# A fused Mamba and feed-forward kernel: z's products around x, softplus without a clamp, u for two tiles at once, and a loop written out

## The chip, the cores and the metric

The kernel runs on one core of one Trainium2 chip. The metric is the device time of one execution in microseconds. The kernel before was timed three times: 2849.44 us at the median, 2845.27 to 2853.36.

## The reference, cut to what matters

The input x has 2 sequences of 2048 rows of 512 numbers. A small recurrence with 64 states gives y0; its layer norm feeds a Mamba block, and a feed-forward block follows (second phase of the kernel, not touched by the change). In the Mamba block, with 1024 inner channels and 16 states each:

```python
xz = xn @ W_in
x_br, z = jnp.split(xz, 2, axis=-1)
xb = jax.nn.silu(conv(x_br) + conv_b)          # causal, 4 taps
Bm = xb @ W_b;  Cm = xb @ W_c
delta = jax.nn.softplus(xb @ W_delta + b_delta)
A_bar = jnp.exp(delta[..., None] * A)
Bx = delta[..., None] * Bm[:, :, None, :] * xb[..., None]
h = A_bar * h + Bx                             # scan over time
y = jnp.sum(h * Cm[:, None, :], axis=-1) + xb * Dp
out = y * jax.nn.silu(z) @ W_out
```

The kernel's u is delta * xb, so that Bx = u * B.

## The kernel before

**Tiling.** Time is cut into NBLK = 16 blocks of T = 256 columns (two sequences in turn), the channels into ND = 8 tiles dt of 128 partitions, the 16 states of a tile into 4 groups g of G = 4. A step k of `scan_phase` works on three blocks at once: it scans block k (`scan`), makes xb, z, B, C and delta of block k + 1 (`front`), and finishes block k - 1 (`back`). Steps run from k = -1 to 16. Each step has NQ = 32 slots q = 4 * dt + g, and each engine has its own written order of jobs by slot: the table `plan` on PE, `next_plan`, `scan_plan`, `turned` and `back_plan` on ACT, `next_plan` and `scan_plan` on DVE.

**A slot.** ACT writes the decay factors exp(delta * A) of group q to PSUM (L659; called exp(q) below; two buffers, so exp(q) waits for scan q - 2). DVE multiplies u by B into a ring of 4 buffers (`bx`, L836, one slot ahead; it waits until PE has turned state q - 4) and scans (`scans`, L844). POOL saves the carry (L445) and multiplies by C in two halves (L452). PE turns the states by transposes that add in PSUM (`turn_states`, L1041). At g = 0 DVE first computes u of the tile in PSUM (L818) and writes column 0 of B (L833, L829). In slots q % 4 = 1 DVE multiplies a finished tile by silu(z) (`gate`, L782), and `turn_gated` (L1051) on PE and `gT` (L592) on ACT turn a pair of such tiles back.

**The next block's work.** PE has two PSUM banks, `work[0]` and `work[1]`, for its products. The order of their users is the order of the table `BANK`; `give(job)` waits until the user before has been copied out. In slots q = 12 to 18 PE makes x (`x(j, m)`, L980, 4 taps each) and z (`z(j)`, L988), ACT copies them out (`xcopy`, L539; `zcopy`, L532) and applies silu to x (L548) before it copies z. `bc` (L996) needs silu of x, then `dl` (L1007) makes delta's argument v in four pairs of tiles.

**Softplus.** It is max(v, ln(1 + min(e^v, CAP))): `dexp` on ACT makes e^v into `lnbuf` (L574) and v into `delta` (L576); `dmin` on DVE clamps `lnbuf` (L765); `dln` on ACT takes Ln(x + 1) (L582); `dmax` on DVE takes the maximum (L772).
**The loop.** `run_steps` runs steps -1, 0, 15 and 16 with constants and steps 1 to 14 as a loop of 7 turns with two steps each, on every engine; SP, which issues the DMAs, loops over steps 1 to 12. In the loop the values waited for are computed in registers from the loop variable.

## Time and profile before

| | |
|---|---|
| median of 3 runs | 2849.44 us |
| profiled execution | 2850.96 us, its span 2848.9 us |
| first scan to last scan | 116 to 2327.6 us of the span |
| second phase | 2327.6 to 2848.9 us |
| busy | PE 2387.0, DVE 2361.8, ACT 1680.4, POOL 1679.7 us |
| granted TensorE clock, mean | 0.915 of 2.4 GHz |

A row of a timeline is: start and duration in us, engine, line, operation, output <- inputs, shape, number of instructions merged into it, and in brackets the idle time of the engine before it with what ended it.
### The profile page before, as it was taken

What the parts mean: (1) busy time and instruction counts of PE and PEld (TensorE: products, weight loads), DVE (VectorE), ACT (ScalarE), POOL (GpSimd) and SP (SyncE); (2) the same over time, 40 slices, a digit from 0 to 9 for tenths busy, and PEclk for the clock granted to TensorE, in tenths of its full rate; (3) what the DMA queues carried; (4) which work ended last, traced back from release to release, by engine and by line L of the source; (5) the groups of instructions that cost most, each with busy time, mean ns of one, the idle gap of its engine ahead of it and who ended that gap; (6) DMA issues with size and microseconds to landing.
All of it is one profiled execution on the core that took longest, in us unless ns stands there. A gap on an engine that the chain in (4) does not pass through costs nothing. (4 is left out here: it accounts for less than half of the span.)

```text
span 2848.9 us, 38192 instructions
## 1 busy us (share of the span) xinstructions
PE 2387.0 (84%) x11520; PEld 1647.4 (58%) x11520; DVE 2361.8 (83%) x2454; ACT 1680.4 (59%) x3282; POOL 1679.7 (59%) x1993
## 2 busy tenths in 40 slices
PE   7878888888878888888888878888888794999997
PEld 5556666565757575757565657565666331444443
DVE  2489898989898989898989899988989664788886
ACT  2566656565756575756575656666666334555554
POOL 0277677767676767676677677676767550223231
PEclk8889999999999898999899999898998896999999
DMA  4101020202020101011010102020102532111110
GB/s 173 67 2 69 7 71 5 72 5 74 2 76 9 68 16 61 19 57 47 30 54 22 62 16 68 8 69 8 60 9 89 216 132 79 49 67 59 62 59 23
DMA packets 47510, 152.50 MB, mean 54 GB/s; under 512 B 7973, under 2 KB 8869, under 8 KB 44206
## 3 DMA queue, kind: packets, MB, share of 16 engines
q1 hardware_dynamic: 47278, 149.76, 14.7%
q8 instruction: 102, 1.67, 0.3%
q14 instruction: 130, 1.06, 0.1%
HBM read 132.37 MB, written 17.37 MB: 53 GB/s over the span
## 5 line engine op out<-in xcount | busy, mean ns | idle before, releaser
L452 POOL TENSOR_TENSOR ring<-ring,Cbc 128x512 f32<-128x512 f32 x1024 | 1290.8, 1282 | 44.2
L844 DVE TENSOR_TENSOR_SCAN ring<-a_ps,ring 128x1024 f32<-128x1024 f32 x512 | 1165.0, 2278 | 25.9 <-ACT a_ps L659 25.9
L659 ACT ACTIVATE a_ps<-delta,nA 128x255 f32<-128x255 f32 x2048 | 854.3, 467 | 506.1 <-DVE ring L844 505.2
L1041 PE MATMUL yT_ps<-ident,ring 128*128 128x128 f32 x4096 | 613.4, 295 | 215.4 <-POOL ring L452 188.6
L1041 PEld LDWEIGHTS yT_ps<-ident,ring 128*128 128x128 f32 x4096 | 501.3, 151 | 320.0 <-POOL ring L452 257.4
L836 DVE TENSOR_TENSOR ring<-u_ps,Bbc 128x1024 f32<-128x1024 f32 x512 | 621.0, 1213 | 76.7 <-PE yT_ps L1041 69.6
L445 POOL TENSOR_TENSOR carry<-ring,half 128x4 f32<-128x4 f32 x512 | 145.2, 284 | 599.0 <-DVE ring L844 595.1
L1007 PE MATMUL work<-xb,big 128*128 128x256 f32 x2048 | 482.2, 389 | 0.0
L1007 PEld LDWEIGHTS work<-xb,big 128*128 128x128 f32 x2048 | 392.6, 197 | 51.3 <-issue 0.4
L980 PE MATMUL work<-y0s,big 128*128 128x256 f32 x1024 | 240.6, 392 | 1.2 <-ACT y0s L512 1.2
L1023 PE MATMUL work<-Wout,xb 128*128 128x512 f32 x512 | 241.3, 607 | 0.0
L1381 POOL TENSOR_TENSOR m<-m,pows 128x1 f32<-128x1 f32 x64 | 34.2, 549 | 310.9 <-DVE m L1513 310.9
L980 PEld LDWEIGHTS work<-y0s,big 128*128 128x128 f32 x1024 | 199.0, 198 | 29.9 <-ACT y0s L512 1.5
L1023 PEld LDWEIGHTS work<-Wout,xb 128*128 128x128 f32 x512 | 98.4, 199 | 112.2 <-issue 112.2
L988 PE MATMUL work<-big,y0s 128*128 128x512 f32 x128 | 85.8, 781 | 67.8 <-ACT zs L532 67.8
L539 ACT ACTIVATE xb<-work,V 128x256 f32<-128x256 f32 x128 | 53.7, 471 | 133.8 <-PE work L980 133.8
L1448 PE MATMUL o_ps<-q,qhT 128*128 128x512 bf16 x512 | 119.3, 387 | 11.8 <-DVE qhT L1546 11.8
L1412 PE MATMUL x_ps<-lay,x2T 128*128 128x512 f32 x256 | 122.0, 621 | 0.7 <-ACT x2T L1473 0.7
L1427 PE MATMUL h_ps<-q,qaT 128*128 128x512 bf16 x512 | 115.7, 379 | 0.0
L574 ACT ACTIVATE lnbuf<-work,V 128x256 f32<-128x256 f32 x128 | 60.4, 472 | 87.2 <-PE work L1007 87.2
L1479 ACT ACTIVATE hb<-hb 128x2048 f32<-128x2048 f32 x32 | 61.2, 1912 | 65.5 <-DVE hb L1532 65.5
L1532 DVE SCALAR_TENSOR_TENSOR hb<-h_ps,m,b1r 128x2048 f32<-128x2048 f32 x32 | 75.2, 2350 | 27.6 <-PE h_ps L1427 27.6
(194 smaller groups left out, 2581.7 us busy)
## 6 DMA issues: line engine op xcount, KB each, us to landing
Bbc<-bc_rows SPq DMA_DIRECT2D x64, 512.0 KB, 4.7
Cbc<-bc_rows SPq DMA_DIRECT2D x64, 512.0 KB, 3.8
xT<-in_xT SPq DMA_DIRECT2D x16, 514.0 KB, 3.2
x_rows<-x2row SPq DMA_DIRECT2D x32, 256.0 KB, 2.0
xp<-x_rows SPq DMA_DIRECT2D x32, 256.0 KB, 2.7
xx<-in_x SPq DMA_DIRECT2D x32, 256.0 KB, 2.9
out_rows<-orow SPq DMA_DIRECT2D x32, 256.0 KB, 2.0
delta<-in_c_w SPq DMA_DIRECT2D x6, 1024.0 KB, 5.1
```

Of the source, the lines that this page charges most:

```text
L445: nc.gpsimd.tensor_tensor(carry[:, par, dt, G * g:G * g + G].rearrange("p (g o) -> p g o", o=1), h[:, :, T - 1:T], ident1, ALU.mult).then_ ...
L452: nc.gpsimd.tensor_tensor(hp, hp, Cbc[:, G * g + GP * c:G * g + GP * c + GP, :], ALU.mult)\
L659: r = nc.scalar.activation(a_ps[q % 2][:, i, 1:T], delta[:, par, dt, 1:T], ACT.Exp, scale=nA[:, dt, s:s + 1])
L836: dve.tensor_tensor(ring[:, q % RING, :, :], u_ps.rearrange("p (a t) -> p a t", a=1).to_broadcast([P, G, T]), Bbc[:, G * g:G * g + G, :], ...
L844: dve.tensor_tensor_scan(ring[:, q % RING, :, :].rearrange("p g t -> p (g t)"), a_ps[q % 2][:, :, :].rearrange("p g t -> p (g t)"), ring[: ...
L980: r = pe.matmul(ps[:, T * m:T * m + T], Mx[:, tap, c:c + P], y0s[:, fp, tap:tap + T], start=(tap == 0), stop=(tap == 3))
L1007: r = pe.matmul(ps[:, T * m:T * m + T], Wd[:, d, c:c + P], xb[:, fp, d, :], start=(d == 0), stop=(d == ND - 1))
L1023: r = pe.matmul(ps[:, :], xb[:, fp, d, P * tt:P * tt + P], Wout[:, d, :], start=False, stop=(d == ND - 1))
L1041: r = pe.matmul(yT_ps[:, tt, :], ring[:, q % RING, i, P * tt:P * tt + P], ident[:, :], is_transpose=True, start=False, stop=(g == NG - 1 a ...
L1412: r = pe.matmul(x3_ps[:, :], x2T[:, d, :], lay[:, batch, d, :], start=(d == 0), stop=(d == KD - 1))
L1427: r = pe.matmul(h_ps[:, 512 * c:512 * c + 512], qaT[:, d, :], q1[:, d, 512 * c:512 * c + 512], start=(d == 0), stop=(d == KD - 1))
L1448: r = pe.matmul(o_ps[:, :], qhT[:, d, :], q2[:, d, :], start=(d == 0), stop=(d == KF - 1))
```

## The change

z(0) and z(1) are made before x, right behind `turn_gated(0)`; z(2) and z(3) stay in slots 17 and 18; the parts of x move back by up to one slot and a half; ACT copies z(0) and z(1) in slot 14 and z(2), z(3) behind silu. `prj` is spread over three slots. Softplus becomes relu(v) + ln(1 + exp(-|v|)): `dexp` makes |v| and relu(v), a new ACT function `dtail` applies exp(-x) to the whole of `lnbuf`, `dmin` is gone, and the maximum becomes an addition. u is made for two tiles in one instruction at the even tiles. The steps of the loop are written out on all engines.

```diff
-        "XB0": 0, "XB1": 1, "XB2": 0, "XB3": 1, "Z0": 0, "Z1": 1, "Z2": 0, "Z3": 1, "GT1": 1, "BC": 1, "DL0": 0,
+        "Z0": 0, "Z1": 1, "XB0": 0, "XB1": 1, "XB2": 0, "XB3": 1, "Z2": 0, "Z3": 1, "GT1": 1, "BC": 1, "DL0": 0,
...
-        u_ps = u_full[:, 0:T]
+        u_ps = u_full[:, :].rearrange("p (m t) -> p m t", m=2)
...
-            with eng.Fori(0, (NBLK - 2) // 2) as i:
-                step(2 * i + 1, 1, True, True, True)
-                step(2 * i + 2, 0, True, True, True)
+            for k in range(1, NBLK - 1):
+                step(k, k % 2, True, True, True)
...
-            with sp.Fori(0, (NBLK - 4) // 2) as i:
-                step(2 * i + 1, 1, True, True, True)
-                step(2 * i + 2, 0, True, True, True)
+            for k in range(1, NBLK - 3):
+                step(k, k % 2, True, True, True)
...
-                        nc.scalar.activation(lnbuf[:, j % 2, T * m:T * m + T], ps[:, T * m:T * m + T], ACT.Exp,
+                        nc.scalar.activation(lnbuf[:, j % 2, T * m:T * m + T], ps[:, T * m:T * m + T], ACT.Abs,
                                              bias=bias).then_inc(s_dexp, 1)
                         r = nc.scalar.activation(delta[:, par if late else fp, mt, :], ps[:, T * m:T * m + T],
-                                                 ACT.Identity, bias=bias)
+                                                 ACT.Relu, bias=bias)
                     r.then_inc(free[BANK[f"DL{j}"]], 1)
+
+                def dtail(pair, late):
+                    b = k if late else n
+                    act.wait_ge(s_dexp, 8 * b + 4 * pair + 4)
+                    nc.scalar.activation(ln_full[:, :], ln_full[:, :], ACT.Exp, scale=-1.0).then_inc(s_dmin, 1)
...
-                next_plan = {5: [prj], 6: [prj_ln], 12: [y0scale], 13: [y0back], 15: [lambda: xcopy(0)],
-                             16: [lambda: xcopy(1)], 17: [lambda: xcopy(2)], 18: [lambda: xcopy(3), silu],
-                             19: [lambda: zcopy(0)], 20: [lambda: zcopy(1), lambda: zcopy(2)], 21: [lambda: zcopy(3)],
-                             22: [bc], 23: [zsilu], 24: [lambda: dexp(0, False)], 26: [lambda: dexp(1, False)],
+                next_plan = {5: [prj], 6: [prj_ln], 12: [y0scale], 13: [y0back], 14: [lambda: zcopy(0), lambda: zcopy(1)], 16: [lambda: xcopy(0)],
+                             17: [lambda: xcopy(1), lambda: xcopy(2)], 18: [lambda: xcopy(3), silu],
+                             19: [lambda: zcopy(2)], 20: [lambda: zcopy(3)],
+                             22: [bc], 23: [zsilu], 24: [lambda: dexp(0, False)], 26: [lambda: dexp(1, False), lambda: dtail(0, False)],
...
-                scan_plan = {1: [lambda: dexp(3, True)], 6: [lambda: dln(1, True)]}
-                turned = {14: 0, 21: 1, 28: 2}
+                scan_plan = {1: [lambda: dexp(3, True), lambda: dtail(1, True)], 6: [lambda: dln(1, True)]}
+                turned = {13: 0, 21: 1, 28: 2}
...
-                def dmin(pair, late):
-                    dve.wait_ge(s_dexp, 8 * (k if late else n) + 4 * pair + 4)
-                    dve.tensor_scalar(ln_full[:, :], ln_full[:, :], CAP, None, ALU.min).then_inc(s_dmin, 1)
...
-                    dve.tensor_tensor(d, d, ln_full[:, :], ALU.max).then_inc(s_delta, 1)
+                    dve.tensor_tensor(d, d, ln_full[:, :], ALU.add).then_inc(s_delta, 1)
...
-                    if g == 0:
+                    if g == 0 and dt % 2 == 0:
...
-                        dve.tensor_tensor(u_ps[:, 1:T], delta[:, par, dt, 1:T], xb[:, par, dt, 1:T], ALU.mult).then_inc(s_u, 1)
+                        dve.tensor_tensor(u_ps[:, :, 1:T], delta[:, par, dt:dt + 2, 1:T], xb[:, par, dt:dt + 2, 1:T],
+                                          ALU.mult).then_inc(s_u, 1)
...
-                        dve.wait_ge(s_u, ND * k + dt + 1)
+                        dve.wait_ge(s_u, ND // 2 * k + dt // 2 + 1)
...
+                        if dt % 2:
+                            dve.wait_ge(s_bx, NQ * k + q)
...
-                                      u_ps.rearrange("p (a t) -> p a t", a=1).to_broadcast([P, G, T]),
+                                      u_ps[:, dt % 2:dt % 2 + 1, :].to_broadcast([P, G, T]),
...
-                             13: [keep_y0], 25: [lambda: dmin(0, False)], 27: [lambda: dmax(0, False)]}
-                scan_plan = {3: [lambda: dmin(1, True)], 7: [lambda: dmax(1, True)]}
+                             13: [keep_y0], 27: [lambda: dmax(0, False)]}
+                scan_plan = {7: [lambda: dmax(1, True)]}
...
-                plan = {0: [("n", prj, 0), ("n", prj, 1)], 1: [("n", prj, 2)],
+                plan = {0: [("n", prj, 0)], 1: [("n", prj, 1)], 2: [("n", prj, 2)],
...
-                        11: [("s", turn_gated, 0, k)], 12: [("n", x, 0, 0), ("n", x, 0, 1)],
-                        13: [("n", x, 1, 0), ("n", x, 1, 1)], 14: [("n", x, 2, 0), ("n", x, 2, 1)],
-                        15: [("n", x, 3, 0), ("n", x, 3, 1)], 16: [("n", z, 0), ("n", z, 1)], 17: [("n", z, 2)],
+                        11: [("s", turn_gated, 0, k)], 12: [("n", z, 0), ("n", z, 1), ("n", x, 0, 0)],
+                        13: [("n", x, 0, 1), ("n", x, 1, 0)], 14: [("n", x, 1, 1), ("n", x, 2, 0)],
+                        15: [("n", x, 2, 1), ("n", x, 3, 0)], 16: [("n", x, 3, 1)], 17: [("n", z, 2)],
```

The wait for the bank of YB, which stood before x, now stands before z(0).

## Rows read from the trace of the kernel before

**Rows 1.** The page, part 1: busy time, share of the span, instructions.

```profile
PE 2387.0 (84%) x11520; PEld 1647.4 (58%) x11520; DVE 2361.8 (83%) x2454; ACT 1680.4 (59%) x3282; POOL 1679.7 (59%) x1993
```

**Rows 2.** Windows, one stretch for a step: steps 3, 8, 9 and 11.

```profile
521.70:661.50 139.80, 117.55 (x574) 88.10 (x573) 124.56 (x110) 86.73 (x186) 97.62 (x116) 0.91 0.11 36
...
1214.50:1351.00 136.50, 115.26 (x574) 86.50 (x573) 124.18 (x109) 86.64 (x186) 97.49 (x116) 0.92 0.12 39
1351.00:1490.90 139.90, 118.58 (x573) 89.62 (x572) 123.59 (x111) 86.64 (x186) 97.65 (x116) 0.90 0.11 38
...
1627.60:1764.40 136.80, 113.26 (x575) 86.23 (x574) 123.54 (x111) 86.52 (x186) 97.59 (x116) 0.95 0.12 41
```

**Rows 3.** Timeline of DVE: end of step 0, of step 8, start of step 9.

```profile
197.47 0.18 DVE L833 TENSOR_REDUCE Bbc<-big 128x16 f32<-128x16 f32 x1 [2.27 <-PE yT_ps L1041]
...
244.39 4.46 DVE L844 TENSOR_TENSOR_SCAN ring<-a_ps,ring 128x1024 f32<-128x1024 f32 x2
...
1346.57 4.46 DVE L844 TENSOR_TENSOR_SCAN ring<-a_ps,ring 128x1024 f32<-128x1024 f32 x2
1352.00 0.43 DVE L818 TENSOR_TENSOR u_ps<-delta,xb 128x255 f32<-128x255 f32 x1 [0.96 <-issue]
```

**Rows 4.** Timeline of PE at the start of step 9.

```profile
1357.19 1.09 PE L1041 MATMUL yT_ps<-ident,ring 128*128 128x128 f32 x8 [3.66 <-issue]
```

**Rows 5.** Groups by line and shape: B's product, Ln, a table load.

```profile
L836 DVE TENSOR_TENSOR ring<-u_ps,Bbc 128x1024 f32<-128x1024 f32 x512 | 621.0, 1213 | 76.7 <-PE yT_ps L1041 69.6
...
L659 ACT ACT_TABLE_LOAD x62 | 79.5, 1283 | 1.1
...
L582 ACT ACTIVATE lnbuf<-lnbuf 128x1024 f32<-128x1024 f32 x32 | 33.7, 1052 | 0.2
```

**Rows 6.** Timeline of DVE in slot q = 3 of step 8.

```profile
1228.06 0.67 DVE L765 TENSOR_SCALAR lnbuf<-lnbuf 128x1024 f32<-128x1024 f32 x1
1228.65 0.43 DVE L818 TENSOR_TENSOR u_ps<-delta,xb 128x255 f32<-128x255 f32 x1
1229.11 0.18 DVE L833 TENSOR_REDUCE Bbc<-big 128x16 f32<-128x16 f32 x1
```

**Rows 7.** Timeline of DVE in step 8, slots 18, 20 and 25.

```profile
1294.56 2.29 DVE L844 TENSOR_TENSOR_SCAN ring<-a_ps,ring 128x1024 f32<-128x1024 f32 x1 [1.48 <-ACT a_ps L659]
...
1299.41 0.18 DVE L833 TENSOR_REDUCE Bbc<-big 128x16 f32<-128x16 f32 x1 [2.24 <-PE yT_ps L1041]
...
1325.56 0.92 DVE L765 TENSOR_SCALAR lnbuf<-lnbuf 128x1024 f32<-128x1024 f32 x1 [1.27 <-ACT lnbuf L574]
...
1326.40 1.21 DVE L836 TENSOR_TENSOR ring<-u_ps,Bbc 128x1024 f32<-128x1024 f32 x1
```

**Rows 8.** Timeline of PE in step 8, slots 12 to 24, and one window.

```profile
1271.34 7.08 PE L980 MATMUL work<-y0s,big 128*128 128x256 f32 x32
...
1288.88 1.88 PE L988 MATMUL work<-big,y0s 128*128 128x512 f32 x4
...
1295.10 2.08 PE L988 MATMUL work<-big,y0s 128*128 128x512 f32 x2 [4.33 <-ACT zs L532]
...
1302.96 3.21 PE L996 MATMUL work<-xb,Wbc 128*32 128x256 f32 x14
...
1324.12 1.91 PE L1041 MATMUL yT_ps<-ident,ring 128*128 128x128 f32 x16
...
1295.10:1301.50 6.40, 5.71 (x14) 3.20 (x15) 4.13 (x5) 4.77 (x11) 2.79 (x3) 0.58 0.00 0
```

**Rows 9.** Timeline of ACT in step 8, slots 18 to 21.

```profile
1287.34 0.84 ACT L539 ACTIVATE xb<-work,V 128x256 f32<-128x256 f32 x2 [1.94 <-PE work L980]
...
1289.55 2.00 ACT L548 ACTIVATE xb<-xb 128x1024 f32<-128x1024 f32 x2
...
1292.86 1.67 ACT L659 ACTIVATE a_ps<-delta,nA 128x255 f32<-128x255 f32 x4
...
1300.85 0.60 ACT L532 ACTIVATE zs<-work 128x512 f32<-128x512 f32 x1 [1.49 <-PE work L988]
```

More of the change, by code:

```diff
@@ L854, in step @@
                         mx_scale()
-                        dve.memset(u_ps[:, 0:1], 1.0).then_inc(s_aclr, 1)
+                        dve.memset(u_ps[:, :, 0:1], 1.0).then_inc(s_aclr, 1)
                         dve.wait_ge(s_mxc, ND)
@@ L972, in x @@
                 def x(j, m):
-                    if j == 0 and m == 0:
-                        pe.wait_ge(free[BANK["YB"]], jobs_before("YB", k) + 1)
-                        if isinstance(k, int) and k == -1:
-                            pe.wait_ge(s_mxc, ND)
                     ps = work[BANK[f"XB{j}"]] if m else give(f"XB{j}")
@@ L985, in z @@
                 def z(j):
+                    if j == 0:
+                        pe.wait_ge(free[BANK["YB"]], jobs_before("YB", k) + 1)
+                        if isinstance(k, int) and k == -1:
+                            pe.wait_ge(s_mxc, ND)
                     ps = give(f"Z{j}")
```

## The prediction

> **What bounds the kernel now.** I read the busy shares first: PE 84%, DVE 83%, the others near 59% [rows 1]. Two engines at about the same share say little, so I cut the span at the ends of the 16 scan steps, which are the ends of the last pair of scans of a step [rows 3], and read each stretch with its granted clock [rows 2]. A step in the middle takes 136.5 us with DVE busy 124.2 and PE 115.3. DVE is therefore the main line, with some 12 us of waits per step. The second phase, behind the scan steps, is not changed.
>
> Then I read DVE's rows with their idle time. In slots q = 0 to 14 it hardly waits. From q = 15 to 25 it waits for PE's turned states, for ACT's exponentials and for the two exponentials that `dmin` clamps [rows 7]. There PE is full: its products run without a pause from 1271.34 to 1290.76 [rows 8], then it idles 4.33 us until ACT has copied z's first product, and ACT copies only behind silu and two table loads [rows 9]. So a step has two parts: DVE sets q = 26 to 31 and 0 to 11, and the chain PE, ACT, PE sets q = 12 to 25.
>
> Last, the step lengths. Step 8 takes 136.5 us, step 9, the first of a turn of the loop, 139.9 [rows 2]. Steps 3, 5, 7 and 13 are like step 9 (139.7 to 139.8), all other looped steps are 136.3 to 136.8, and step 11, also behind a jump, is 136.8 at a clock of 0.95 [rows 2].
>
> **The loop written out.** Six jumps back (before steps 3, 5, 7, 9, 11, 13) go. At a jump DVE stands 0.96 us for "issue" [rows 3] and PE 3.66 us, after which PE starts at half clock [rows 4]. I price the jump by the lengths: 5 steps x (139.8 - 136.55) = 16.3 us, and 0.2 for step 11, 16.5 in all. The low bound is what DVE itself loses at the jump, 6 x 0.96 = 5.8 us, in case the rest is half-clock time that turns up elsewhere; I take 16.5, because the even steps have no jump and are all short. The wait values become constants. Step 0 already has constants: from q = 20's column to its end it takes 248.85 - 197.47 = 51.4 us [rows 3], step 8 takes 1351.03 - 1299.41 = 51.6 [rows 3, 7]. So constants give 0 to 0.2 us per step, and I take 0; the register arithmetic is hidden by the busy engine.
> The Trainium skill ("Runtime: NRT & Kernel Launch", Instruction fetch mechanics) says that fetch runs ahead in sequence and a taken branch away from it stalls. The two stalls agree; by that rule straight code costs nothing extra, and the sum stays.
>
> **DVE: softplus without the clamp.** Two `dmin` go per step. The one in q = 3 costs 1228.65 - 1228.06 = 0.59 us of DVE [rows 6]. The one in q = 25 costs 0.84 and the wait of 1.27 before it, 2.1 us [rows 7]; what is late next is PE's turn of state 22, so this part is worked out below. `max` becomes `add` of the same operands: no row shows an add, the product of 1024 elements takes 1.21 us [rows 5], and I take the add to cost what the maximum did: 0 (-0.1 to 0.1).
>
> **DVE: u for two tiles.** A u costs 1229.11 - 1228.65 = 0.46 us [rows 6], busy 0.43 for 255 elements; the product of 1024 takes 1.21 [rows 5], so an element costs (1.21 - 0.43) / 769 = 1.0 ns and 255 more cost 0.26: 0.72 for a double one. Bounds are one u (0.46) and two (0.92). In q = 0 to 11: +0.27 -0.46 +0.27 -0.46 = -0.4 us. With `dmin` -0.6, so DVE reaches q = 12 1.0 us sooner (0.6 to 1.4). The doubles in q = 15 and 23 lie in waits for PE; the one missing in q = 27 gives 0.46. The new wait of an odd tile is for a product two scans old and holds nothing.
>
> **ACT.** `Exp` becomes `Abs` and `Identity` becomes `Relu`, same sizes: 0. No row shows either; Identity and Copy run between exponentials without a table load, and a load would be 1.28 us [rows 5] (rival 3). Added is `dtail`, an Exp of 128x1024, priced by the Ln of that size, 1.05 us [rows 5]; 0.70 to 1.1. In q = 1 exp(1) is behind it, which scan(1) wants only after scan(0) and a product: hidden. In q = 26 behind it stand exp(26), which DVE's scan(26) needs, and Ln, which DVE's add needs in q = 27. `dmin` began when the last Exp of `dexp` ended, at 1325.56 [rows 7]; Relu 0.35, `dtail` 1.05, exp(26) 1.67, load 1.28 and Ln 1.05 end at 1331.0. DVE, with bx(26) at 1325.2 (below), has gate 0.4, two scans of 2.2 and a product of 1.2 to do and reaches the add at 1332.4. Hidden by 1.4 us; a shift of PE's product shifts both. If the cover is gone, `dtail` costs its 1.05 us.
>
> **PE and ACT: z around x.** All times here are of step 8, with the 1.0 us gained earlier set aside. z(0), z(1) (1.9 us) move in front of x; x(3,1) then ends where z(1) ended, at 1290.76 [rows 8], instead of 1287.3. zcopy(0), zcopy(1) now stand before exp(14) and end about 1273.8, so exp(14) ends 1275.5, before scan(14) starts: hidden by 0.7 us. The cost is silu. xcopy(3) 0.84, load 1.28, silu 2.00, load 1.28, exp(18) 1.67 [rows 5, 9] (7.07 together, and gaps of 0.1) put scan(18) at 1297.9 instead of 1294.56 [rows 7]. Then zcopy(2) 0.58, exp(19) 1.66, zcopy(3) 0.60: 1300.8. z(2) and z(3) no longer wait and are done by 1294.1, but turn_gated(1) is behind z(3) on PE and its bank is free only at 1300.8, formerly 1301.45 [rows 9]. exp(20) and the copy gT(1) then let bc start at 1303.1, formerly 1302.96 [rows 8]. So the 4.33 us wait is replaced by one of 6.7 us at the next product, and bc starts 0.15 us later.
> Clock: behind the 4.33 us idle the stretch 1295.1 to 1301.5 has 0.58 [rows 8], so z(2), turn 16 and z(3) ran mostly at 1.2 GHz. In the new order they run at 2.4 GHz and the slow time falls on turn 17 and on bc (3.64 us at full clock), which nothing hides. At 0.58, some 5.4 of the 6.4 us were slow. As much from 1300.8 on reaches 1306.2, 3.1 us into bc, a loss of 1.5. Bounds: 0, if the clock does not fall, to 3.4, if it stays low for some 9 us. x may also meet slow time sooner: 0.3 (0 to 1).
> The Trainium skill ("TensorE: Matmul & The Clock Gate", Part 1) says that idleness gates the clock and activity releases it. The row agrees, and by it the longer idle speaks against this edit.
> From bc on PE has no pause to q = 25. Turns 22 and 23 ran from 1324.12 on for 1.91 us [rows 8], so turn 22 ended at about 1325.2, and bx(26) started behind `dmin` at 1326.40 [rows 7]. Now bx(26) starts when turn 22 ends, 1.2 sooner but for what PE loses. A step gains 1.0 (before q = 12) + 1.2 + 0.46 (u of q = 27) - 0.15 (bc) = 2.5 us, less the slow time of 1.5 + 0.3: 0.7 us. Bounds: 2.5, and -1.9 with 3.4 + 1 us of slow time.
>
> **prj and the rest.** `prj`'s parts go to q = 0, 1, 2. The load of the next xT on SP starts a slot later, a step before its use; ACT takes prj in q = 5: 0. gT(0) in q = 13 waits for PE until about 1267.3 while scan(11) still runs: 0. Step -1: bc about 2 us sooner, but the table load for Exp now comes after Abs, 1.28 + 0.35 later: 0 (-2 to 2). Step 15 (no z, x): -0.8.
>
> **Sum.** 16.5 + 15 x 0.7 + 0.8 = 27.8 us. Span 2848.9 becomes 2821.1; the profiled run took 2850.96 (2.1 around the span), so 2823.2. That run is 1.5 over the median 2849.44, so 2821.7, rounded 2822.
>
> **Rivals.** (1) The clock doesn't fall behind the longer idle, or falls where work is hidden: 2.5 us per step, 2849.4 - 16.5 - 37.5 - 0.8 = 2795. For: steps with other slow places differ by 3 us (step 11 at 0.95). Against: PE's 4.33 us idle has slow work behind it in step 8, and the new one is longer. (2) Slower: silu is late, in q = 18. PE idles 6.7 us or more before turn_gated(1) and stays slow through bc into `dl`, which DVE waits for. At 3.4 + 1 us of slow time and 1 us by which exp(17), behind xcopy(2), holds back scan(17), a step loses 2.9: 2849.4 - 17.3 + 43.5 = 2876. From a loss of 1.15 us per step on it outweighs the jumps. For: the row of 0.58 [rows 8]. Against: exp(17) has some 1.2 us to spare. (3) The change doesn't do what it says: Abs or Relu cost table loads, two of 1.28 around each `dexp`. In q = 26 the add waits 1.2 us and exp(27) another 0.8: 15 x 2 = 30 us, and we are at 2852. The Trainium skill ("ScalarE: Activation LUTs", Table sets) lists both beside exp, which speaks against this rival. (4) The step's gain is given back in full and only the jumps count: 2832. (5) Straight code stalls on fetch, or the jumps' half-clock time comes back: 5.8 + 11.3 = 17 us, 2832 to 2843.
>
> **Chances.** Forecast 0.42 (2806 to 2832), rival 1 0.18, rival 2 0.08, rival 3 0.06, rival 4 0.14, rival 5 0.12. A measurement tells about 0.3% (8.5 us), so faster means under 2840.9. Faster: 0.42 + 0.18 + 0.14 + 0.07 = 0.81; same: 0.05 of rival 5, 0.04 of rival 3, 0.02 of rival 2 = 0.11; slower 0.08. The range leaves out rivals 2 and 3 and the far end of 1: 2789 to 2845.
>
> **What would show it.** No "issue" wait at a step's start, and all of steps 1 to 14 alike, at 135.8 us. No DVE row for the clamp, four u of about 0.7 us per step. PE without a wait at z, but 6 to 7 us idle before turn_gated(1), and a clock near 0.6 in the stretch behind it. DVE's wait before scan(18) near 5 us. Wrong would be: table loads at the Abs line, steps shorter than 134.5, or bc running at full clock.

## The result and the profile of the changed kernel

| | before | changed |
|---|---|---|
| device time, median (lowest to highest) | 2851.4 us (2845.27 to 2853.76) | 2809.86 us (2808.35 to 2811.09) |
| ratio, 95% interval | | 0.9857 [0.9839, 0.9875] |
| profiled execution | 2850.96 us | 2811.04 us |
| its span, mean granted clock | 2848.9 us, 0.915 | 2808.1 us, 0.922 |

The change makes the kernel 41 us faster. The windows of the changed kernel answer to those of [rows 2]: step 0, step 8, step 9, all of steps 1 to 14, step 15 and the second phase. The columns are the stretch, its length, the busy time (and instructions) of PE, PEld, DVE, ACT and POOL, the granted clock, the share of DMA and GB/s.

```profile
109.00:246.50 137.50, 110.42 (x540) 87.20 (x539) 120.60 (x103) 90.92 (x195) 95.15 (x117) 0.83 0.07 23
1189.60:1325.00 135.40, 114.99 (x577) 86.33 (x577) 122.03 (x105) 88.34 (x188) 97.60 (x116) 0.92 0.13 42
1325.00:1459.30 134.30, 112.69 (x571) 85.27 (x570) 122.06 (x105) 88.23 (x188) 97.69 (x116) 0.94 0.11 41
246.50:2134.80 1888.30, 1593.09 (x8015) 1200.96 (x8014) 1708.49 (x1443) 1236.04 (x2632) 1366.33 (x1611) 0.93 0.12 40
2134.80:2287.10 152.30, 117.37 (x483) 56.96 (x482) 119.48 (x98) 71.28 (x159) 95.38 (x113) 0.87 0.50 184
2287.10:2808.10 521.00, 436.98 (x2113) 214.54 (x2143) 364.27 (x646) 276.29 (x275) 118.73 (x138) 0.94 0.16 55
```

The same windows of the kernel before that were not shown yet: step 0, steps 1 to 14, step 15.

```profile
109.00:248.80 139.80, 111.43 (x551) 88.09 (x550) 123.30 (x110) 89.63 (x193) 95.41 (x117) 0.84 0.07 23
...
248.80:2177.20 1928.40, 1626.14 (x8010) 1225.17 (x8009) 1735.63 (x1528) 1212.64 (x2604) 1366.11 (x1611) 0.92 0.11 39
...
2177.20:2327.60 150.40, 117.24 (x490) 57.08 (x489) 121.18 (x102) 70.44 (x158) 95.43 (x113) 0.88 0.49 187
```

Of the 40.8 us of span, steps 1 to 14 give 1928.4 - 1888.3 = 40.1 and the stretch of step 0 gives 139.8 - 137.5 = 2.3; step 15 takes 152.3 - 150.4 = 1.9 back. The long steps of 139.8 us are gone: steps 1 to 13 now take 134.2 or 134.3 and 135.4 in turn, step 14 takes 136.2.

What took the place of the old waits in slots 17 to 22 stands in three timelines of step 8: DVE, PE and ACT. Square brackets hold the idle time ahead of an instruction and what ended it. PE's last two lines and DVE's last one are of step 9.

```profile
1263.64 2.28 DVE L846 TENSOR_TENSOR_SCAN ring<-a_ps,ring 128x1024 f32<-128x1024 f32 x1
...
1271.99 2.29 DVE L846 TENSOR_TENSOR_SCAN ring<-a_ps,ring 128x1024 f32<-128x1024 f32 x1 [4.96 <-ACT a_ps L662]
...
1283.30 1.22 DVE L838 TENSOR_TENSOR ring<-u_ps,Bbc 128x1024 f32<-128x1024 f32 x1 [2.18 <-PE yT_ps L1043]
...
1417.57 1.23 DVE L838 TENSOR_TENSOR ring<-u_ps,Bbc 128x1024 f32<-128x1024 f32 x1 [1.05 <-PE yT_ps L1043]
```

```profile
1266.52 1.02 PE L990 MATMUL work<-big,y0s 128*128 128x512 f32 x2
...
1274.60 1.12 PE L1053 MATMUL work<-ident,gbuf 128*128 128x128 f32 x4 [7.06 <-ACT zs L530]
...
1277.35 4.88 PE L998 MATMUL work<-xb,Wbc 128*32 128x256 f32 x16
...
1410.00 1.11 PE L1053 MATMUL work<-ident,gbuf 128*128 128x128 f32 x4 [7.06 <-ACT zs L530]
...
1412.75 3.54 PE L998 MATMUL work<-xb,Wbc 128*32 128x256 f32 x15
```

```profile
1264.77 0.84 ACT L537 ACTIVATE xb<-work,V 128x256 f32<-128x256 f32 x2 [2.81 <-PE work L978]
...
1266.98 2.00 ACT L546 ACTIVATE xb<-xb 128x1024 f32<-128x1024 f32 x2
...
1270.30 1.67 ACT L662 ACTIVATE a_ps<-delta,nA 128x255 f32<-128x255 f32 x4
...
1273.97 0.58 ACT L530 ACTIVATE zs<-work 128x512 f32<-128x512 f32 x1
```

ACT does xcopy(3), silu and exp(18) in a row, so DVE stands 4.96 us before scan(18), where it stood 1.48 [rows 7]. z(2) runs without a wait, in 1.02 us where it took 2.08 behind one [rows 8], but PE then stands 7.06 us before turn_gated(1), where it stood 4.33 before z(2) [rows 8]. Behind that idle time bc's sixteen products take 4.88 us in step 8 and 3.76 in step 9 (3.54 for the fifteen shown), and DVE's wait before bx(22) is 2.18 us in the one and 1.05 in the other. That is the whole difference between the two step lengths.

The waits of the whole kernel say the same: total us, times, longest.

```profile
PE work L1053 <- ACT zs L530: 105.9, 15, 7.1
...
DVE ring L846 <- ACT a_ps L662: 77.9, 17, 5.0
```

The groups of the softplus and of u (busy us, mean ns, idle time before):

```profile
L817 DVE TENSOR_TENSOR u_ps<-delta,xb 128x510 f32<-128x510 f32 x64 | 54.7, 855 | 0.0
L662 ACT ACT_TABLE_LOAD x62 | 79.5, 1283 | 1.1
L581 ACT ACTIVATE lnbuf<-lnbuf 128x1024 f32<-128x1024 f32 x32 | 34.3, 1072 | 0.0
```

The table loads are 62 as before [rows 5], so Abs and Relu load nothing. A double u takes 0.855 us in the mean; the first of a step is the slow one (1.43 us in step 8, median of all 0.68).

### The profile page after: what moved, and what is told of

The parts are those of the page before. It is cut to its first block and busy times, and to the rows that moved or that the text cites. A ratio compares the mean times of both kernels' runs of the same rounds, so it can differ in the third digit from the quotient of the medians.

```text
span 2808.1 us, 34215 instructions
## 1 busy us (share of the span) xinstructions
PE 2345.5 (84%) x11488; PEld 1623.8 (58%) x11520; DVE 2330.2 (83%) x2358; ACT 1707.3 (61%) x3314; POOL 1679.8 (60%) x1993
## 5 line engine op out<-in xcount | busy, mean ns | idle before, releaser
L1043 PEld LDWEIGHTS yT_ps<-ident,ring 128*128 128x128 f32 x4096 | 495.4, 149 | 289.1 <-POOL ring L450 253.3
L978 PE MATMUL work<-y0s,big 128*128 128x256 f32 x1024 | 233.1, 380 | 0.0
L978 PEld LDWEIGHTS work<-y0s,big 128*128 128x128 f32 x1024 | 189.4, 190 | 35.3 <-ACT zs L530 10.4
L1053 PE MATMUL work<-ident,gbuf 128*128 128x128 f32 x256 | 51.1, 334 | 123.8 <-ACT zs L530 105.9
L1450 PE MATMUL o_ps<-q,qhT 128*128 128x512 bf16 x481 | 112.0, 386 | 18.9 <-DVE qhT L1548 18.7
L1053 PEld LDWEIGHTS work<-ident,gbuf 128*128 128x128 f32 x256 | 35.6, 169 | 140.8 <-ACT zs L530 118.3
```

What stands on the lines that cost most here:

```text
L978: r = pe.matmul(ps[:, T * m:T * m + T], Mx[:, tap, c:c + P], y0s[:, fp, tap:tap + T], start=(tap == 0), stop=(tap == 3))
L1043: r = pe.matmul(yT_ps[:, tt, :], ring[:, q % RING, i, P * tt:P * tt + P], ident[:, :], is_transpose=True, start=False, stop=(g == NG - 1 a ...
L1450: r = pe.matmul(o_ps[:, :], qhT[:, d, :], q2[:, d, :], start=(d == 0), stop=(d == KF - 1))
```

## The experiments

All kernels but the ones compared by name are timed against the kernel before. Runs 1 to 4 share a chip (before: 2845.1 us), so do 5 to 8 (2843.8) and 9 to 12 (2851.8). For all of them the last columns are of steps 1 to 14 in the profiled execution, divided by 14: the length of a step, DVE's busy time, the rest of the step, in which DVE is idle, and the time at half clock, which is the length times twice what the mean granted clock lacks to 1.

| kernel | median us | ratio, 95% interval | step | DVE busy | DVE idle | half clock |
|---|---|---|---|---|---|---|
| before | 2851.4 | | 137.7 | 124.0 | 13.8 | 21.7 |
| changed | 2809.9 | 0.9857 [0.9839, 0.9875] | 134.9 | 122.0 | 12.8 | 18.5 |
| e1 loop written out alone | 2833.4 | 0.9954 [0.9932, 0.9977] | 136.5 | 124.2 | 12.3 | 20.5 |
| e2 changed, with the loop | 2826.6 | 0.9931 [0.9905, 0.9957] | 136.5 | 122.2 | 14.3 | 20.5 |
| e3 changed, z in its old place | 2780.3 | 0.9768 [0.9734, 0.9801] | 133.1 | 122.1 | 11.0 | 12.7 |
| e4 e1 and z moved | 2883.3 | 1.0128 [1.0094, 1.0161] | 139.9 | 124.2 | 15.8 | 27.3 |
| e5 e1 and softplus | 2832.7 | 0.9958 [0.9936, 0.998] | 136.3 | 122.8 | 13.5 | 19.5 |
| e6 e1 and u | 2828.4 | 0.9958 [0.9943, 0.9973] | 136.3 | 123.6 | 12.7 | 20.2 |
| e7 changed, silu a slot later | 2782.3 | 0.9797 [0.9777, 0.9816] | 133.1 | 122.1 | 11.0 | 13.4 |
| e8 e7 and turn_gated(1) later | 2789.1 | 0.982 [0.9799, 0.9841] | 133.4 | 122.1 | 11.3 | 17.8 |
| e9 changed, idle products | 2798.7 | 0.982 [0.9801, 0.984] | 134.5 | 122.1 | 12.4 | 11.9 |
| e10 e1, idle products | 2828.5 | 0.9924 [0.9905, 0.9942] | 135.8 | 124.2 | 11.6 | 17.3 |
| e11 e5, idle products | 2811.3 | 0.9865 [0.9846, 0.9884] | 135.0 | 122.7 | 12.3 | 15.6 |
| e12 e3, idle products | 2774.5 | 0.9731 [0.9715, 0.9748] | 132.5 | 122.2 | 10.3 | 11.0 |

Where DVE is idle, from the same traces: the mean per step of steps 1 to 14, in us, by the scan that comes next. The last column is the sum of all other places.

| kernel | scans 14, 15 | scan 18 | scan 19 | scans 20, 21 | elsewhere |
|---|---|---|---|---|---|
| before | 1.8 | 1.5 | 2.0 | 1.2 | 7.3 |
| changed | 0.8 | 5.0 | 0.0 | 1.5 | 5.6 |
| e1 | 1.9 | 1.5 | 1.5 | 1.2 | 6.3 |
| e3 | 0.8 | 1.5 | 2.1 | 1.1 | 5.6 |
| e4 | 2.4 | 5.0 | 0.1 | 2.1 | 6.3 |
| e5 | 2.6 | 1.5 | 2.3 | 1.2 | 5.9 |
| e6 | 1.6 | 1.5 | 2.5 | 1.2 | 5.9 |
| e7 | 0.7 | 0.0 | 1.5 | 3.2 | 5.6 |
| e9 | 1.6 | 5.0 | 0.0 | 0.3 | 5.6 |
| e10 | 2.2 | 1.5 | 0.3 | 1.4 | 6.3 |
| e12 | 1.3 | 1.5 | 0.5 | 1.5 | 5.6 |

Ahead of scans 14 and 15 stand PE's first products of x, ahead of scan 18 ACT's exponential behind silu, ahead of scan 19 z's products, ahead of scans 20 and 21 turn_gated(1) and bc. DVE makes the column and the product of a slot one slot ahead, so its wait before bx(22) is in the column of scans 20, 21.

Medians of different chips are not compared without their ratios: from the changed kernel to e7, for one, the medians say 27.6 us and the ratios 0.0060 x 2850 = 17; the profiled spans say 2808.1 - 2779.1 = 29.0.

### The loop, alone and taken back

**e1**, the kernel before with the loop written out:

```
-            with eng.Fori(0, (NBLK - 2) // 2) as i:
-                step(2 * i + 1, 1, True, True, True)
-                step(2 * i + 2, 0, True, True, True)
+            for k in range(1, NBLK - 1):
+                step(k, k % 2, True, True, True)
...
```

> The kernel before with the loop written out and nothing else. Theory of the forecast: six jumps of 3.2 us each (less for one) go and constants give nothing, so 2851.4 - 16.5 = 2835, every step 1 to 14 at 136.5 us, no wait for issue at a step's start. Rival: only DVE's 0.96 us per jump is a true cost and the rest is half-clock time that falls elsewhere: 2851.4 - 5.8 = 2845.6, some steps still near 139.8. Second rival: constants speed every step too: below 2828.

The span goes from 2848.9 to 2832.5 us, by 16.4, and the median from 2845.1 to 2833.4, by 11.7 on this chip, where the kernel before ran between 2829 and 2855 (0.0046 x 2850 = 13 by the ratio). The looped steps are alike within 0.6 us (136.2 to 136.8), as expected; one window, step 8:

```profile
1203.90:1340.40 136.50, 115.81 (x574) 87.32 (x573) 124.14 (x111) 86.41 (x186) 97.40 (x116) 0.92 0.12 41
```

**e2**, the changed kernel with the loop put back (the same lines, the other way round):

> The changed kernel with the loop put back and nothing else. Forecast's theory: the parts add up, the jump costs what it cost before, 2809.9 + 16.5 = 2826, with steps in two lengths 3.2 us apart. Rival: the new order has slack or sets its lengths by half-clock time in another way, so that a jump costs only the 0.96 us of DVE: 2816 or less.

It is 16.8 us slower than the changed kernel by the medians (2826.6 against 2809.9; 0.0074 x 2850 = 21 by the ratios; 2827.2 - 2808.1 = 19.1 by the spans). The jumps thus cost 12 to 16 us in the kernel before and 17 to 21 in the changed one: of one size, and not told apart more finely than that. Two lengths of steps 3.2 us apart were expected and don't show: steps take 135.7 to 137.7 us.

Where the price sits can be read from the kernel before. In its steps 3, 5, 7, 9 and 13 DVE is idle 3.7 us more than in the same steps of e1: 1.2 at the jump itself, 0.7 in slot 3, and 0.9 and 0.7 ahead of scans 15 and 19, which wait for PE. In step 11, behind a jump as well, the last two waits are 0.8 and 1.6 us in all (in e1 1.8 and 1.5), and the step takes only 136.8 us. So most of what a jump costs is lost behind it, in waits for PE.

### z in its old place, and z moved alone

**e3**, the changed kernel with z, x, their copies, gT(0) and prj where they were:

```
-                        11: [("s", turn_gated, 0, k)], 12: [("n", z, 0), ("n", z, 1), ("n", x, 0, 0)],
-                        13: [("n", x, 0, 1), ("n", x, 1, 0)], 14: [("n", x, 1, 1), ("n", x, 2, 0)],
-                        15: [("n", x, 2, 1), ("n", x, 3, 0)], 16: [("n", x, 3, 1)], 17: [("n", z, 2)],
+                        11: [("s", turn_gated, 0, k)], 12: [("n", x, 0, 0), ("n", x, 0, 1)],
+                        13: [("n", x, 1, 0), ("n", x, 1, 1)], 14: [("n", x, 2, 0), ("n", x, 2, 1)],
+                        15: [("n", x, 3, 0), ("n", x, 3, 1)], 16: [("n", z, 0), ("n", z, 1)], 17: [("n", z, 2)],
...
```

> The changed kernel with x, z, their copies, gT(0) and prj in their old places; softplus, u and the written-out loop stay. Theory A (forecast): the move of z trades a PE wait of 4.3 us for one of 7 us, bc starts at the same time, so the move gives nothing or costs its half-clock time; this kernel comes out between 2797 and 2812, with PE waiting 4.3 us before z(2) and DVE 1.5 us before scan(18). Rival B: the move is where the step's gain comes from; this kernel is at 2820 or above.

The kernel is 30 us faster than with z moved (2780.3 against 2809.9; 25 by the ratios), where theory A had 2797 to 2812 and rival B 2820 or more: both missed. The move of z is the part of the change that costs, and more than either allowed. A step of e3, DVE's wait before scan(18), and PE's before z(2):

```profile
1175.90:1309.50 133.60, 113.50 (x575) 85.82 (x573) 122.13 (x105) 88.20 (x189) 97.50 (x116) 0.95 0.12 44
```

```profile
1255.61 2.29 DVE L846 TENSOR_TENSOR_SCAN ring<-a_ps,ring 128x1024 f32<-128x1024 f32 x1 [1.48 <-ACT a_ps L662]
```

```profile
1256.15 1.46 PE L990 MATMUL work<-big,y0s 128*128 128x512 f32 x2 [4.33 <-ACT zs L530]
```

DVE does the same work as in the changed kernel (122.1 us a step) and is idle 1.9 us less. PE's idle time before z(2) is the old 4.33 us, yet z(2) takes 1.46 us behind it and not 2.08 [rows 8], and a step has 12.7 us at half clock, where the changed kernel has 18.5.

**e4**, e1 with the same lines moved the other way:

> The kernel before with the loop written out and x, z, their copies, gT(0) and prj in their new places; softplus and u as before. Theory A: 2835 to 2850, no faster than the written-out loop alone. Rival B: at least 10 us below the written-out loop alone, 2825 or less.

It is 50 us slower than e1 on the same chip, and the only kernel slower than before; 2835 to 2850 was expected, a miss on the same side as e3's. A step, and PE behind its longer wait:

```profile
1228.20:1368.10 139.90, 116.84 (x574) 87.16 (x572) 124.14 (x110) 86.47 (x186) 97.35 (x116) 0.90 0.12 42
```

```profile
1315.67 1.12 PE L1049 MATMUL work<-ident,gbuf 128*128 128x128 f32 x4 [7.06 <-ACT zs L530]
...
1318.42 5.26 PE L994 MATMUL work<-xb,Wbc 128*32 128x256 f32 x16
```

bc takes 5.26 us, 1.6 more than at full clock, and half-clock time rises from 20.5 to 27.3 us a step. DVE's idle time rises by 3.4 us a step, 14 x 3.4 = 48 us: 2.0 of it ahead of scans 18 and 19 together (silu's place), 0.9 ahead of scans 20 and 21 (bc) and 0.5 ahead of scans 14 and 15.

### The two edits of DVE, each alone

**e5**, e1 with Abs, Relu, `dtail` and `add` in the place of Exp, Identity, `dmin` and `max`:

```
-                             13: [keep_y0], 25: [lambda: dmin(0, False)], 27: [lambda: dmax(0, False)]}
-                scan_plan = {3: [lambda: dmin(1, True)], 7: [lambda: dmax(1, True)]}
+                             13: [keep_y0], 27: [lambda: dmax(0, False)]}
+                scan_plan = {7: [lambda: dmax(1, True)]}
...
```

> The kernel before with the loop written out and softplus without a clamp (dexp, dtail, add; no dmin); x, z and u as before. Forecast: 0.6 us from q = 3 and up to 1.2 us from q = 25 per step, 15 steps: 9 to 27 us below the written-out loop alone. Rival (half-clock time takes it back): less than 5 us below it. Second rival: Abs and Relu cost table loads, which the groups would show with more than 62 loads at the exponentials' line.

Its ratio is that of e1, so the forecast of 9 to 27 us missed and the rival of less than 5 holds. DVE works 1.4 us less per step and is idle 1.2 us more: 0.7 more ahead of scan 15, 0.8 more ahead of scan 19 (z's products) and 0.4 less at the place of `dmin`. In slot 15 of the longer steps DVE stands 3.00 us ahead of its column, in e1 2.03 (the rows say issue; on PE the turn that it needs stands behind x's first products). The stretch before it, in which these run, has a clock of 0.69. A step and that stretch of e5, its slot 15, and the slot 15 of e1:

```profile
1205.70:1342.40 136.70, 115.87 (x575) 87.20 (x574) 122.79 (x109) 88.32 (x188) 96.86 (x116) 0.93 0.12 43
...
1255.50:1272.00 16.50, 14.71 (x63) 12.50 (x64) 13.69 (x11) 8.29 (x22) 13.85 (x17) 0.69 0.00 1
```

```profile
1272.19 0.18 DVE L832 TENSOR_REDUCE Bbc<-big 128x16 f32<-128x16 f32 x1 [3.00 <-issue]
```

```profile
1269.98 0.18 DVE L831 TENSOR_REDUCE Bbc<-big 128x16 f32<-128x16 f32 x1 [2.03 <-issue]
```

**e6**, e1 with u for two tiles at once:

```
-                    if g == 0:
+                    if g == 0 and dt % 2 == 0:
...
-                        dve.tensor_tensor(u_ps[:, 1:T], delta[:, par, dt, 1:T], xb[:, par, dt, 1:T], ALU.mult).then_inc(s_u, 1)
+                        dve.tensor_tensor(u_ps[:, :, 1:T], delta[:, par, dt:dt + 2, 1:T], xb[:, par, dt:dt + 2, 1:T],
+                                          ALU.mult).then_inc(s_u, 1)
...
```

> The kernel before with the loop written out and u for two tiles; the rest as before. Forecast: 0.4 us before q = 12 and 0.46 in q = 27, 15 steps: 13 us below the written-out loop alone, and about 1 us more of DVE freed in step 15. Rival: the double u is slower than 0.72 us (its mean in the changed kernel is 0.855) and the rest lies in waits: 0 to 6 us below it.

Again the ratio of e1, so the forecast of 13 us missed and the rival of 0 to 6 holds: DVE works 0.6 us less per step and is idle 0.4 more, of which 1.0 more ahead of scan 19. The two edits alone are worth 0.7 and 5 us by the medians (chips differ; by the ratios nothing either time), together, as e3 has them over e1 on one chip, 53. They don't add up. The half-clock time differs: 19.5 and 20.2 us a step apart, 12.7 together. So does DVE's idle time ahead of scans 14 and 15, where x's products run: 2.6 and 1.6 us apart, 0.8 together.

### silu behind exp(18)

**e7** leaves PE's order as the change has it and moves ACT's xcopy(3) and silu behind exp(18):

```
-                             17: [lambda: xcopy(1), lambda: xcopy(2)], 18: [lambda: xcopy(3), silu],
-                             19: [lambda: zcopy(2)], 20: [lambda: zcopy(3)],
+                             17: [lambda: xcopy(1), lambda: xcopy(2)], 19: [lambda: xcopy(3), silu],
+                             20: [lambda: zcopy(2), lambda: zcopy(3)],
```

> The changed kernel with xcopy(3) and silu behind exp(18) instead of before it, and zcopy(2), zcopy(3) together in slot 20. Theory (what sets slots 18 to 21 is ACT's silu before exp(18)): DVE's wait of 4.96 us before scan(18) goes, one of about 1.1 us comes before scan(19), PE's wait of 7.06 us before turn_gated(1) becomes 5.5, bc starts 1.5 to 2 us sooner: 1 to 2 us per step, 2780 to 2796. Rival (PE's products and their half-clock time set these slots): PE starts bc no sooner and the time stays at 2805 to 2812.

It takes 2782.3 us, within the theory's 2780 to 2796. A step, DVE before scan(19), its wait for an exponential now, and PE before turn_gated(1):

```profile
1173.80:1306.90 133.10, 111.14 (x575) 83.87 (x574) 122.13 (x105) 88.09 (x188) 97.62 (x116) 0.96 0.12 43
```

```profile
1256.18 2.29 DVE L846 TENSOR_TENSOR_SCAN ring<-a_ps,ring 128x1024 f32<-128x1024 f32 x1 [1.43 <-ACT a_ps L662]
```

```profile
1257.20 1.11 PE L1053 MATMUL work<-ident,gbuf 128*128 128x128 f32 x4 [5.47 <-ACT zs L530]
```

So one change in ACT's plan gives back what z's move cost: DVE's 4.96 us before scan(18) is gone and 1.43 before scan(19) and 1.6 before bx(21) come in, PE's 7.06 becomes 5.47, and a step is as short as with z in its old place, no shorter. z's move costs with silu ahead of exp(18) and gains nothing without it. Half-clock time falls too, from 18.5 to 13.4 us a step, so this run changes the order and the clock at once; e9 below changes the clock alone. Whether silu behind exp(18) would also help with z in its old place was not run.

**e8** moves, on top of e7, turn_gated(1) and its copy from slot 18 to the next:

```
-                turned = {13: 0, 21: 1, 28: 2}
+                turned = {13: 0, 20: 1, 28: 2}
...
-                        18: [("n", z, 3), ("s", turn_gated, 1, k)], 19: [("n", bc)],
+                        18: [("n", z, 3)], 19: [("s", turn_gated, 1, k), ("n", bc)],
```

> As the one before, and turn_gated(1) on PE goes behind turn 17 into slot 19, its copy gT(1) on ACT into slot 20. Theory: turn 17 no longer stands behind the wait for zcopy(3), and PE's idle time is cut in two parts, which also leaves less half-clock time in bc: another 0.5 to 1.5 us per step, 2765 to 2790. Rival: turn 17 was never late for DVE and bc waits for the same copy: equal to the one before within 3 us.

PE's idle time before turn_gated(1) shrinks to 3.50 us, and nothing is gained: 2789.1 against 2782.3 on the same chip, inside the stated range but slower where 0.5 to 1.5 us a step were to be gained, so the theory missed, half-clock time 17.8 instead of 13.4 us a step, bc 5.16 us. A shorter wait of PE is not by itself less time at half clock. Why bc is slower behind a wait of 3.50 us than behind 7.06 in the changed kernel's step 9 was not found out.

### Keeping PE at work in its wait

These four kernels compute all that the reference wants and add products of 256 columns into a half of yT's bank that nothing reads. They test whether the clock, and not the order, costs the time: they give PE more to do and take no wait away.

```
-        yT_ps = pb("yT_ps", [P, NT, P])
+        yT_full = pb("yT_ps", [P, 512])
+        yT_ps = yT_full[:, 0:T].rearrange("p (t c) -> p t c", t=NT)
...
+                def warm(n, dt):
+                    wait(pe, s_gate, ND * k + dt)
+                    for _ in range(n):
+                        pe.matmul(yT_full[:, T:2 * T], ident[:, :], Mx[:, 0, 0:T], start=False, stop=False,
+                                  skip_group_check=True)
...
-                        18: [("n", z, 3), ("s", turn_gated, 1, k)], 19: [("n", bc)],
+                        18: [("n", z, 3), ("w", warm, 13, 4), ("s", turn_gated, 1, k)], 19: [("n", bc)],
```

**e9**, the changed kernel with thirteen of them before turn_gated(1), as above:

> The changed kernel with 13 products of 256 columns (5.8 us, into the unused half of yT's PSUM bank, read by nobody) put on PE behind z(3), in the 7.06 us in which it waits for zcopy(3). Theory (half-clock time behind this idle stretch is what the move of z costs): bc runs at full clock and each step is 0.5 to 1.5 us shorter, 2786 to 2804, though PE has 78 us more work. Rival (the order of the waits costs it): work added to PE gives nothing or delays, 2808 or more.

It takes 2798.7 us, 11 less than the changed kernel by the medians and by the ratios. The stretch of bc, PE, and DVE at bx(22):

```profile
1270.00:1276.00 6.00, 5.36 (x30) 3.24 (x31) 6.00 (x4) 3.94 (x11) 5.10 (x6) 1.00 0.00 0
```

```profile
1262.87 5.78 PE L1052 MATMUL yT_ps<-big,ident 128*128 128x256 f32 x26
...
1270.09 0.66 PE L1060 MATMUL work<-ident,gbuf 128*128 128x128 f32 x4 [1.45 <-ACT zs L531]
...
1272.17 3.64 PE L999 MATMUL work<-xb,Wbc 128*32 128x256 f32 x16 [0.54 <-ACT xb L596]
```

```profile
1276.87 1.22 DVE L839 TENSOR_TENSOR ring<-u_ps,Bbc 128x1024 f32<-128x1024 f32 x1 [0.25 <-PE yT_ps L1044]
```

bc runs at full clock in 3.64 us, the clock of the stretch is 1.00, and DVE's wait before bx(22) falls from 2.18 and 1.05 to 0.25 us. DVE's 4.96 us before scan(18) stays, since that is ACT's. Only 5.9 us of the gain lie in steps 1 to 14 (1888.3 to 1882.4), 0.4 us a step where 0.5 to 1.5 were expected: ahead of scans 20 and 21 DVE is idle 1.3 us less a step, and ahead of scans 14 and 15 0.8 more. Step 15 gives 2.9 more (152.3 to 149.4).

e9 has less half-clock time than e7 (11.9 against 13.4 us a step) and yet a step is 1.4 us longer. So of the 1.8 us a step between the changed kernel and e7 the filled wait alone brings 0.4, and the rest hangs on silu's place.

**e10** is e1 with eight of them before z(2):

```
-                        15: [("n", x, 3, 0), ("n", x, 3, 1)], 16: [("n", z, 0), ("n", z, 1)], 17: [("n", z, 2)],
+                        15: [("n", x, 3, 0), ("n", x, 3, 1)], 16: [("n", z, 0), ("n", z, 1)], 17: [("w", warm, 8, 4), ("n", z, 2)],
```

> The kernel before with the loop written out and 8 such products (3.6 us) on PE before z(2), in its wait of 4.33 us. Theory: z(2), turn 16 and z(3) run at full clock, PE is 1 to 2 us sooner at bc, steps go from 136.5 to 133 to 135.5: 2785 to 2820. Rival: 2830 or more.

It takes 2828.5 us, where 2785 to 2820 was expected: a miss. z(2) does run at full clock (1.12 us for 2.08), and DVE is idle 1.2 us less ahead of scan 19, but slow time comes earlier in most steps, within x, where slot 15's wait becomes 2.48 us. Half-clock time falls from 20.5 to 17.3 us a step only, and DVE's idle time by 0.7.

**e11** is e5 with three of them before turn_back and two before turn_gated(0), ahead of x:

```
-                        9: [("n", turn_y0), ("b", wout, 1, 2)], 10: [("n", turn_back)],
-                        11: [("s", turn_gated, 0, k)], 12: [("n", x, 0, 0), ("n", x, 0, 1)],
+                        9: [("n", turn_y0), ("b", wout, 1, 2)], 10: [("w", warm, 3, 2), ("n", turn_back)],
+                        11: [("w", warm, 2, 2), ("s", turn_gated, 0, k)], 12: [("n", x, 0, 0), ("n", x, 0, 1)],
```

> The kernel with the written-out loop and the new softplus alone (2832.7), with 3 products of 256 columns before turn_back and 2 before turn_gated(0), the waits in front of x. Theory: that kernel lost its gain in x, which ran at half clock for up to 10 us and held DVE 3.0 us in q = 15; with the clock kept up x runs at full clock, DVE waits 0.8 us there, and the clamp's 1 to 2 us per step show: 2795 to 2820. Rival: the gain is lost by an order of waits, and the time stays at 2830 to 2837.

It takes 2811.3 us, within the expected range, 21 less than e5 by the medians (27 by the ratios). Steps take 133.5 and 136.1 us, and the difference is slot 15's wait, 0.79 us in the short ones and 2.48 in the long ones:

```profile
1187.10:1320.60 133.50, 113.07 (x576) 85.21 (x575) 122.65 (x108) 88.20 (x188) 96.72 (x116) 0.96 0.12 41
1320.60:1456.70 136.10, 118.30 (x592) 88.77 (x591) 122.58 (x108) 88.31 (x188) 96.69 (x116) 0.94 0.11 39
```

```profile
1251.31 0.18 DVE L833 TENSOR_REDUCE Bbc<-big 128x16 f32<-128x16 f32 x1 [0.79 <-DVE u_ps L818]
```

Against e1 a step is now 1.5 us shorter with the same idle time, which is about the DVE time that softplus saves (1.4). That reading is not shown to the end: e1 with the same five products and the old softplus was not run, so what the products alone would give is open.

**e12** is e3 with both sets:

> The fastest so far, the changed kernel with x and z in their old places (2780), with both sets of added products: 5 in front of x, 8 before z(2). Theory: its remaining 14 us of half-clock time per step, most of it in front of and inside x and z, go, and steps fall from 133.1 to 130 to 132: 2740 to 2768. Rival: DVE is near its own floor (122 us busy) and PE's added work collides: 2775 to 2790.

It takes 2774.5 us, the fastest of all, 0.9731 [0.9715, 0.9748] of the kernel before, and 6 us below e3 by the medians (10 by the ratios); 2740 to 2768 was expected if the 14 us of half-clock time went: a miss, and by the step lengths (132.5, where 130 to 132 were expected) as well. But that time did not go; it falls from 12.7 to 11.0 us a step. DVE gains 1.6 us ahead of scan 19 and loses 0.9 ahead of scans 15, 20 and 21. So this run does not show what a step without half-clock time would take. What is left of DVE's 10.3 us of idle time per step are mostly waits for PE's turns and for the exponential of slot 18.

## Why the prediction was right, and which of its terms were not

The forecast was 2822 us in 2789 to 2845; the kernel takes 2809.9. The direction, the price of the jumps and the new waits in slots 18 to 22 were right. The gain of DVE's edits was taken too small, the price of z's move came out right by luck, from wrong parts, and step 15 had the wrong sign.

**The jumps: right in size.** 16.5 us forecast; alone they measure 16.4 by the spans, 13 by the ratio and 11.7 by the medians (e1), as the last of all edits 19.1, 21 and 16.8 (e2). All lie above the low bound of 5.8: the half-clock time at the jumps doesn't turn up elsewhere. Constants in the waits gave nothing, as taken: e1's steps are as long as the even ones before.

One row was read wrongly there: PE does not start at half clock behind the jump. The eight turns of [rows 4] take 1.09 us, at full clock; eight in a stretch at 0.50 take 1.92 us (changed kernel, step 8, right behind turn_gated(1)). The clock falls only as these turns end. The stretch of the turns and the one behind it:

```profile
1357.10:1358.40 1.30, 1.21 (x10) 1.19 (x11) 1.27 (x3) 0.70 (x2) 0.51 (x2) 1.00 0.26 88
1358.40:1361.90 3.50, 3.50 (x10) 2.81 (x9) 3.46 (x5) 1.33 (x4) 2.39 (x3) 0.51 0.00 0
```

The price did not rest on that reading; it was taken from the lengths of the steps.

**z around x: right in its rows, and in its price by luck.** Scan(18) was to start 3.3 us later, less 1.0 gained before. It started at 1271.99 - 1189.60 = 82.4 us of its step, before at 1294.56 - 1214.50 = 80.1 [rows 2, 7]: 2.3 later, as worked out. The wait of 5 us is 4.96, the 6.7 us of PE are 7.06, and bc starts at 1277.35 - 1189.60 = 87.75 us of the step, 0.7 sooner than before, with 1.0 gained ahead of it. The forecast took 1.5 + 0.3 + 0.15 = 1.95 us a step for the move. Against e3 it costs 134.9 - 133.1 = 1.8, and in step 0 and step 15 another 5. What the forecast had wrong is what this is made of. It put 1.8 of the 1.95 on the clock. But bc loses only 4.88 - 3.64 = 1.2 us to the clock in one kind of step and 0.1 in the other, x loses nothing, and DVE's idle time ahead of scans 20 and 21 rises by 0.5 us. The other 1.4 us stand ahead of scans 18 and 19: silu's place, which the forecast held to be hidden by PE's own lateness, and which e7 gives back. Two errors of about one size cancelled. Alone (e4) the move costs 3.4 us a step, nearly twice the price, and there bc does lose the 1.6 us that the forecast had.

**The other edits' gain: the term that was mis-sized.** The forecast had 1.0 + 1.2 + 0.46 = 2.66 us a step for softplus and u: 2.3 of DVE's work (0.6 + 0.4 + 0.84 + 0.46) and 0.36 of waiting. With z in its old place they give 136.5 - 133.1 = 3.4 (e1, e3): 2.1 of work and 1.4 of waiting. The work was right within 0.2, although the first u of a step takes 1.43 us and not 0.72. The waiting was not. The 0.36 of slot 25 came, and 0.3 more in slot 23; but ahead of scans 14 and 15, where the forecast had these edits change no wait, it falls by 1.1 us (and ahead of scan 19 it rises by 0.6). Half-clock time falls from 20.5 to 12.7 us a step. The forecast had treated the clock as something that only the longer idle time changes, not DVE's sooner starts. So a step gains 3.4 - 1.8 = 1.6 us over the jumps, as (1911.2 - 1888.3) / 14 = 1.6 says, and not 2.66 - 1.95 = 0.7. Beyond e1, whose steps 1 to 14 take 1911.2 us, they gave 1911.2 - 1888.3 = 22.9 us instead of 14 x 0.7 = 9.8, which is the 12 us by which the forecast was high and a little more. All steps were to be alike, at 135.8; they alternate between 134.2 and 135.4, so the mark set for "wrong" (steps under 134.5, bc at full clock) was passed, or nearly so, by every second step. There the kernel comes near rival 1 in number, with 136.5 - 134.2 = 2.3 us gained where it had 2.5, though by other parts: silu's place costs there too.

**Softplus and table loads: right.** No load at the Abs line, `dtail` 1.07 us for 1.05, and `dln` and the add behind it hidden: only one wait of the add is left in the kernel, at its start. The Trainium skill's list of table sets ("ScalarE: Activation LUTs", Table sets), which has abs and relu beside exp, agrees with the 62 loads. Rival 3 is out. But `dmin`'s 0.6 us of q = 3 show in the step only beside the edit of u: alone (e5) the waits ahead of scans 15 and 19 take them back.

**Step 15: wrong.** -0.8 forecast, +1.9 measured. In the fourteen kernels it takes from 149.1 to 154.8 us: with 37.5 us of half clock in it 149.1 to 152.0, with 41.0 152.3 to 154.5, with 44.4 152.2 to 154.8. It goes roughly with the half-clock time, though the ranges overlap, and not with DVE's work, which fell by 1.7 us. What sets the clock there was not tried.

**Rivals.** Rival 2, that silu is late, had the right place, but its price for the move was too high: 0.15 + 4.4 + 1 = 5.55 us a step, where 3.4 were measured alone (e4) and 1.8 in the change. That e4's 2883 us lie near its 2876 is chance, since it had worked that out with the gains of the other edits in it. Its delay of scan(17) by exp(17) doesn't show: DVE's wait ahead of scan 17 is 0.91 us a step before and after. That silu's place is the cause of most of the loss is shown by e7 and e9 together; that half-clock time behind the wait is the cause of a part by e9.

**Open.** Mean steps gather at a few lengths: 136.3 to 136.5 us in e1, e2, e5 and e6, whose DVE work differs by 2.0 us a step, and 133.1 to 133.4 in e3, e7 and e8, whose half-clock time differs by 5. So a small edit can change nothing, and two together more than their sum. Why they do so, why steps come in two lengths, and why e8 has more half-clock time than e7 with less idle time, isn't settled by these runs. They show that half-clock time moves between x, z(2) and bc as edits shift PE's work, but not what decides where it falls.

## What to carry to other kernels

What an edit saves on the critical engine can be lost in its next waits for an engine that runs at half clock there (1.4 us of work saved and 1.2 of waiting added in e5); so read the granted clock behind each idle stretch of PE, and don't judge such edits one by one (0.7 and 5 us alone, 53 together). Before moving work to another place, ask which instruction of a third engine ends up behind it: here silu with its two table loads, put 2.3 us later, stood before an exponential that DVE wanted next and held it up 4.96 us; one slot on it cost 1.4. Price a change also without each of its parts: the part that took away PE's wait before z(2) was the one that cost 25 to 30 us.
